# SyncE fetches the rows of ten tiles in one stream, 14 a step, in place of nine tiles with 13 rows a step

## The chip, the cores and the metric

One core of one Trainium2 chip. The metric is the time of the program on the device in microseconds (us), from the first to the last instruction with what lies around it. Lower is better. The engines are TensorE (PE; PEld is its weight load), VectorE (DVE), ScalarE (ACT), GpSimd (POOL) and SyncE (SP). A q behind a name (SPq, ACTq) means work of the sequencer, such as the issue of a DMA.

## What is computed

One layer of a graph network, its residual, and a layer norm. There are 6250 nodes of 128 features and 106250 edges of 64 features, sorted by target node.

```python
ef = relu(edge_attr @ We1 + be1) @ We2 + be2
ef = ef * sigmoid(timestamps[:, None] @ Wt + bt)
combined = concatenate([x[src], ef], axis=1)
msg = relu(combined @ Wn1 + bn1) @ Wn2 + bn2
out = segment_sum(msg, dst, num_segments=6250) + x
return layernorm(x + out)            # over the 128 features
```

## The kernel before

**Node table.** The part of Wn1 that acts on x[src] is applied to nodes, not to edges: `node_table` = x @ Wn1[:128] + bn1, one row of 128 float32 (512 bytes) a node. It is written to DRAM at the start. Wn2 is applied after the segment sum.

**Tiles.** A tile is 128 edges, one a partition. Four tiles are a group of 512 edges, two groups are a pair, and a pair is one step of the main loop. There are 104 pairs (`PAIRS`). The first four take their rows straight from x (gathered at the start), and the pairs 4 to 103 gather them from the node table. The buffer `gathered` holds four pairs (`BODY` = 4).

**Who does what in step s.** TensorE transposes the edge attributes of pair s into psT (L854, semaphore `eaT_ps`), sums the messages of pair s - 3 (L836), multiplies for pair s - 2 (L877), and makes the two edge layers of pair s (L890) and pair s - 1 (L902). ScalarE, in this order: copies sums, rectifies pair s - 3 (L621), places a fetched tile of pair s - 1 where there is one (`place_rows`, L598 and L602), copies the transposes (L655, `eaT_ready`, for which the first layer of this step and the transposes of the next wait), makes the sigmoid weights `tw` (L679), and rectifies the first layer (L687). VectorE adds the gathered rows of pair s - 2 (L1156, `pre_ready`), builds one-hot matrices and accumulates. In the steps that are multiples of four, ScalarE also stages a finished block of nodes (L715), and TensorE multiplies it in the step after.

**POOL** issues one indirect DMA for each tile, 128 rows each (L528), eight a pair. From pair 20 on (`CLOSE_FROM`) it begins pair p once L1156 of pair p - 2 is done (L539). One tile of some pairs, the last of its second group, is left out by POOL. The pairs in `FETCHED` (17, 27, ... 97, nine of them) have it fetched by SyncE, those in `ACT_FETCHED` (32, 54, 76, 98) by ScalarE's queue.

**SyncE** runs the steps n = 4 to 103 in the loop at the end of its program: wait until the transposes of step n - 4 are done, load the edge attributes of pair n (L438); `fetch_rows(n)`; wait until `tw` of step n - 4 is done, load the edge weights of pair n (L444). `fetch_rows` reads the node numbers of up to 13 edges into registers with one register load (`numbers_of`, L399) and issues for each edge a DMA of its own with one row of 512 bytes (L500). A tile takes the ten steps from p - 6 to p + 3, nine with 13 rows and one with 11. Steps 11 to 100 have rows. There are two buffers of one tile (`fetched`). Tile f waits at its first row until tile f - 2 has been placed (`placed`). `place_rows` on ScalarE waits for the 128 rows, which end in SyncE's step p + 3, and copies them into `gathered` in ScalarE's step p + 1. SyncE's loop runs up to four steps ahead of TensorE.

Of the kernel before, what the change touches and what calls it, by code (L numbers as in the profile page):

```python
# [43 lines left out]
SP_ENGINE = mybir.EngineType.SP  # L44

P = 128
# [30 lines left out]
CLOSE_FROM = 20  # L77


FETCH_ROWS, FETCH_STEPS = 13, 10  # L80
FETCHED = list(range(17, 98, FETCH_STEPS))


ACT_ROWS, ACT_STEPS, ACT_FROM = 6, 22, 10
# [3 lines left out]
def gnn_kernel(nc, x, src, dst, edge_attr, edge_weight, We1, be1, We2, be2, Wt, bt, Wn1, bn1, Wn2, bn2, out):  # L88
# [24 lines left out]
    table = nc.dram_tensor("node_table", (N, C), F32).ap()  # L113
    spans_dram = nc.dram_tensor("spans_dram", (G, 2), I32).ap()

    with ExitStack() as ctx:
        def sb(name, shape, dt=F32):
            return ctx.enter_context(nc.sbuf_tensor(name, shape, dt))
# [4 lines left out]
        def sem(name):  # L123
            return ctx.enter_context(nc.semaphore(name))
# [44 lines left out]
        fetched = sb("fetched", [P, 2, C])  # L169
# [47 lines left out]
        rows_in = [sem(f"rows_in{i}") for i in range(2)]  # L217
        placed, act_placed = sem("placed"), sem("act_placed")
# [74 lines left out]
        def wait_table(eng):  # L293

            for r, n in enumerate((RING, RING, len(BLOCKS) - 2 * RING)):
                eng.wait_ge(table_out[r], 16 * n)
# [99 lines left out]
        def numbers_of(engine, p, parts):  # L396

            g = p * PAIR + PAIR - 1
            return nc.values_load_multi_w_load_instructions(  # L399
                src_rows[g % P:g % P + 1, g // P, :].rearrange("a (p j) -> a j p", j=TILES)  # L400
                [:, ORDER[TILES - 1], parts.start:parts.stop], engines=(engine,), min_val=0, max_val=N - 1,
                skip_runtime_bounds_check_because="the edge's source node, which the inputs bound")[1]

        def by_group(a):

            return [a[E - SE:E].rearrange("(g e) -> g e", e=GE),
                    a[0:(P - SG) * GE].rearrange("(g e) -> g e", e=GE),
                    a[(P - SG) * GE:(G - SG) * GE].rearrange("(g e) -> g e", e=GE)]

        col, row = "(c a) -> c a", "(a c) -> a c"  # L410
# [11 lines left out]
        @block.sync  # L422
        def _(sp):
            def load_x(c):
                sp.dma_start(x_sb[:, c * XCH:(c + 1) * XCH, :],
                             x_blocks[:, c * XCH:(c + 1) * XCH, :]).then_inc(x_in[c], 16)

            def load_rows(tile, a, landed):
                last, first, second = by_group(a)
                for to, of in ((tile[0:SG, 0, :], last), (tile[SG:P, 0, :], first), (tile[0:ROWS[1], 1, :], second)):  # L430
                    sp.dma_start(to, of).then_inc(landed, 16)

            def edges_of(n):

                return (E - SE if n < 2 else (n // 2 - 1) * SE) + n % 2 * PE2

            def load_edges(n):
                sp.dma_start(ea[n // 2 % 2][:, n % 2 * PAIR:(n % 2 + 1) * PAIR, :],  # L438
                             edge_attr[bass.ds(edges_of(n), PE2), :].rearrange("(g p j) f -> p g (j f)", p=P, j=TILES))\
                    .then_inc(ea_in[n % BODY], 16)  # L440

            def load_weights_of(n):

                sp.dma_start(ew[n // 2 % 2][:, n % 2 * PAIR:(n % 2 + 1) * PAIR, :].rearrange("p g e -> p (g e)"),  # L444
                             edge_weight[bass.ds(edges_of(n), PE2)].rearrange("(a e) -> a e", a=1).to_broadcast([P, PE2]))\
                    .then_inc(ew_in[n % BODY], 16)

            def load_raw_e(n, a, b):

                part = src[E - SE:E] if a < SG else src[0:SE]  # L450
                sp.dma_start(raw_e[:, a:b, :], part.rearrange("(g p j) -> p g j", p=P, j=TILES)
                             [:, a % SG:(b - 1) % SG + 1, :]).then_inc(raw_e_in[n], 16)

            load_raw_e(0, 0, 2)
            for c in range(CHUNKS):
                load_x(c)
                if c == 1:
                    load_raw_e(1, 2, 4)
                if c == 3:
                    load_raw_e(2, 4, 8)  # L460
                    load_rows(src_rows, src, src_in)
            sp.dma_start(x_sb[0:LAST, FULL, 0:C], x_last).then_inc(x_in[CHUNKS], 16)
            load_rows(dst_rows, dst, dst_in)
            for to, of in loads_sp:
                sp.dma_start(to, of).then_inc(weights_in, 16)

            for b, (rows, n) in enumerate(BLOCKS):
                sp.wait_ge(table_ready, b + 1)
                sp.dma_start(table_blocks[:, b, :] if b < FULL else table_last,
                             table_sb[b][0:rows, 0:n * C]).then_inc(table_out[min(b // RING, 2)], 16)  # L470
                if b == RING:
                    load_edges(0)
                    load_edges(1)
            load_weights_of(0)
            load_weights_of(1)
            sp.wait_ge(span_ready, 2)
            for r in range(2):
                sp.dma_start(spans_dram[r * P:r * P + ROWS[r], :], span_i[0:ROWS[r], r, :]).then_inc(span_out, 16)
            load_edges(2)
            load_edges(3)  # L480
            sp.wait_ge(span_out, 32)
            sp.dma_start(spans[:, :, :], spans_dram.rearrange("(a g) k -> a g k", a=1)).then_inc(spans_in, 16)
            for to, of in loads_late:
                sp.dma_start(to, of).then_inc(late_in, 16)
            load_weights_of(2)
            load_weights_of(3)

            def fetch_rows(n):

                f, at = divmod(n - (FETCHED[0] - FETCH_STEPS + 4), FETCH_STEPS)  # L490
                if not 0 <= f < len(FETCHED) or at * FETCH_ROWS >= P:
                    return
                if f == 0 and at == 0:
                    wait_table(sp)
                if at == 0 and f > 1:
                    sp.wait_ge(placed, f - 1)
                parts = range(at * FETCH_ROWS, min((at + 1) * FETCH_ROWS, P))
                rows = numbers_of(SP_ENGINE, FETCHED[f], parts)
                for part, row in zip(parts, rows):
                    sp.dma_start(fetched[part:part + 1, f % 2, :], table[bass.ds(row, 1), :])\  # L500
                        .then_inc(rows_in[f % 2], 16)

            for n in range(BODY, PAIRS):
                sp.wait_ge(eaT_ps, n - BODY + 1)
                load_edges(n)
                if n == BODY:
                    sp.wait_ge(src_in, 48)
                fetch_rows(n)
                sp.wait_ge(tw_ready, n - BODY + 1)
                load_weights_of(n)  # L510
            sp.wait_ge(last.y_done, 1)
            sp.dma_start(out_last, x_sb[0:LAST, FULL, 0:C]).then_inc(y_out, 16)
# [3 lines left out]
        def _(pool):  # L516
# [20 lines left out]
            for p in range(RAW // PAIR, PAIRS):  # L537
# [6 lines left out]
                for q in range(PAIR):  # L544
                    for t in range(TILES):
                        if p in FETCHED + ACT_FETCHED and q * TILES + t == PAIR * TILES - 1:
                            continue
                        if p < PAIRS - 1:
                            landed = gather_in[p % BODY][0 if q * TILES + t < PART[0] else 1]
                        else:  # L550
                            landed = last_gather_in[0 if q == 0 else 1 + t]
                        gather_rows(gathered[:, p % BODY * PAIR + q, t * C:(t + 1) * C], table,
                                    src_e[:, p * PAIR + q, t:t + 1], landed,
                                    32 if p in FETCHED + ACT_FETCHED and q * TILES + t == PAIR * TILES - 2 else 16)


        @block.scalar
        def _(act):
# [32 lines left out]
            def place_rows(p):  # L591

                act.wait_ge(pre_ready, p - (BODY - 1))
                to = gathered[:, p % BODY * PAIR + PAIR - 1, (TILES - 1) * C:TILES * C]
                if p in FETCHED:
                    f = FETCHED.index(p)
# [889 lines left out]
```

## Time and profile before

| | us |
|---|---|
| median of 3 runs | 1047.69 (1046.63 to 1048.53) |
| the profiled execution | 1049.1 |
| its span | 1047.3 |
| TensorE busy | 855.0 (82%) |
| GpSimd busy | 779.7 (74%) |
| VectorE busy | 650.6 (62%) |
| ScalarE busy | 593.6 (57%) |
| mean granted clock of TensorE | 0.951 of full speed |

Busy time leaves out instructions that only wait, branch, load registers or issue DMAs. SyncE does nothing else, so it has no line here, and its work is seen only in the timeline. A row of a timeline merges instructions of one line that follow each other: its first number is the start, its second the time from the first's start to the last's end. The idle time in brackets is that ahead of the row, with what ended it.

### The profile page before, as it was taken

The numbers are of one execution on the slowest core, as the hardware profiler recorded it, in microseconds if no ns is written. First come the engines' busy times: TensorE is split into PE (matmuls) and PEld (weight loads), VectorE is DVE, ScalarE is ACT, GpSimd is POOL, SyncE is SP. The second block draws the span as 40 slices with busy tenths as digits, with TensorE's granted clock in tenths as the row PEclk, the third lists the DMA queues.
The fourth block names the chain that finished last, engine by engine and source line by source line (L and its number), as shares of the span: only waits on it lengthen the run. The fifth ranks groups of instructions, "written<-read, shape, count | busy, mean of one in ns | idle before, by whom it ended". The sixth has DMA issues, their size and how long they took to land.

```text
span 1047.3 us, 20873 instructions
## 1 busy us (share of the span) xinstructions
PE 855.0 (82%) x5031; PEld 624.6 (60%) x5032; DVE 650.6 (62%) x1688; ACT 593.6 (57%) x662; POOL 779.7 (74%) x828
## 2 busy tenths in 40 slices
PE   6999997988688888678778887887787786786884
PEld 6667675656566666465565655555565564564664
DVE  4767774765555765655466566566566556566566
ACT  5576664665365656555555555555565555654652
POOL 7777777777777777777777777777777777777773
PEclk9999998999888989989999999999999999999998
DMA  8964445444454444444444544444444444554321
GB/s 244 281 222 123 145 145 142 128 146 145 142 147 127 143 154 145 125 142 146 145 125 146 145 142 146 125 144 138 130 144 138 133 143 127 144 143 145 84 54 50
DMA packets 81709, 148.80 MB, mean 142 GB/s; under 512 B 20631, under 2 KB 50134, under 8 KB 81574
## 3 DMA queue, kind: packets, MB, share of 16 engines
q1 hardware_dynamic: 51750, 89.86, 27.6%
q0 software_dynamic: 26208, 53.73, 19.1%
q10 hardware_dynamic: 3616, 3.74, 1.1%
q8 instruction: 45, 0.74, 0.3%
q14 instruction: 90, 0.74, 0.2%
HBM read 140.85 MB, written 6.40 MB: 141 GB/s over the span
## 4 chain that ended last, share of the span: by engine, by line
POOL 47%; issue 22%; PE 13%; DMA 7%; DVE 6%; ACT 3%; ACTq 1%; SPq 1%; DVEq 1%; POOLq 0%
POOL gathered L528 47%; DMA gathered<-node_table,src_e 6%; PE psS L836 4%; PE psM L877 3%; DVE h L1156 2%; PE psE L902 2%; PE psH L890 2%; DMA x_sb<-in_x 1%; ACT h L621 1%; ACT tw L679 1%; DVE onehot L1162 1%; DVE efw L1177 1%; ACTq L617 0%; PE psS L821 0%; ACT h L687 0%
## 5 line engine op out<-in xcount | busy, mean ns | idle before, releaser
L528 POOL DMA_INDIRECT gathered<-node_table,src_e x787 | 748.0, 950 | 240.9 <-issue 234.1
L687 ACT ACTIVATE h<-psH,be_c 128x1024 f32<-128x1024 f32 x104 | 115.9, 1115 | 332.3 <-PE psH L890 329.3
L836 PE MATMUL psS<-onehot,h 128*128 128x128 f32 x1656 | 235.9, 300 | 76.1 <-ACT h L621 73.6
L836 PEld LDWEIGHTS psS<-onehot,h 128*128 128x128 f32 x1656 | 217.9, 211 | 94.9 <-issue 56.0
L1156 DVE TENSOR_TENSOR h<-psM,gathered 128x1024 f32<-128x1024 f32 (+1 forms) x104 | 122.7, 1182 | 227.9 <-DMA gathered<-node_table,src_e 169.6
L679 ACT ACTIVATE tw<-ew,bt_c,wt_c 128x1024 f32<-128x1024 f32 x104 | 235.5, 2265 | 18.1 <-DVE efw L1177 17.7
L877 PE MATMUL psM<-wn,efw 128*128 128x128 f32 x1664 | 210.6, 282 | 3.2 <-DVE h L1156 3.2
L902 PE MATMUL psE<-h,we 128*128 128x512 f32 x416 | 210.5, 629 | 0.0
L877 PEld LDWEIGHTS psM<-wn,efw 128*128 128x128 f32 x1664 | 203.1, 199 | 4.0 <-DVE h L1156 4.0
L1177 DVE SCALAR_TENSOR_TENSOR efw<-psE,be_c,tw 128x1024 f32<-128x1024 f32 x104 | 133.2, 1281 | 107.3 <-PE psE L902 106.7
L1162 DVE TENSOR_SCALAR onehot<-split_ids,dst_e 128x65 f32<-128x65 f32 x832 | 174.0, 272 | 0.0
L890 PE MATMUL psH<-eaT,we 64*128 64x512 f32 x416 | 121.1, 659 | 56.2 <-DMA gathered<-node_table,src_e 50.0
L902 PEld LDWEIGHTS psE<-h,we 128*128 128x128 f32 x416 | 72.4, 194 | 132.6 <-issue 132.6
L621 ACT ACTIVATE h<-h 128x1024 f32<-128x1024 f32 (+1 forms) x108 | 110.4, 1025 | 36.7 <-DVE h L1156 34.7
L1170 DVE TENSOR_REDUCE found<-onehot 128x128 f32<-128x512 f32 x104 | 109.9, 1056 | 3.6
L854 PEld LDWEIGHTS psT<-ident,ea 128*128 128x128 f32 x416 | 51.9, 141 | 53.0 <-issue 53.0
L890 PEld LDWEIGHTS psH<-eaT,we 64*128 64x128 f32 x416 | 31.8, 187 | 71.5 <-DMA gathered<-node_table,src_e 57.2
L1120 DVE TENSOR_TENSOR acc<-acc,found 128x128 f32 x204 | 58.3, 286 | 24.8 <-issue 18.2
L655 ACT ACTIVATE eaT<-psT 128x512 f32<-128x512 f32 x104 | 61.5, 591 | 7.9 <-PE psT L854 5.1
L854 PE MATMUL psT<-ident,ea 128*128 128x128 f32 x416 | 62.4, 273 | 0.0
L821 PE MATMUL psS<-wn,staged_own 128*128 128x128 f32 x88 | 20.2, 314 | 35.0 <-ACT h L621 35.0
L821 PEld LDWEIGHTS psS<-wn,staged_own 128*128 128x128 f32 x88 | 14.4, 205 | 39.8 <-issue 39.8
(113 smaller groups left out, 342.1 us busy)
## 6 DMA issues: line engine op xcount, KB each, us to landing
ew<-in_edge_weight SPq DMA_DIRECT2D x104, 512.0 KB, 4.2
ea<-in_edge_attr SPq DMA_DIRECT2D x104, 256.0 KB
fetched<-node_table SPq DMA_DIRECT2D x1152, 0.5 KB
gathered<-node_table,src_e POOLq DMA_INDIRECT x787, 2.5
raw_own<-node_table ACTq DMA_DIRECT2D x512, 0.5 KB
x_sb<-in_x SPq DMA_DIRECT2D x6, 512.0 KB, 8.9
out_y<-x_sb ACTq DMA_DIRECT2D x12, 256.0 KB
node_table<-gathered SPq DMA_DIRECT2D x7, 256.0 KB, 5.2
```

The source lines that it names most:

```text
L528: pool.indirect_dma_start(to, None, rows, bass.IndirectOffsetOnAxis(index, 0)).then_inc(landed, by)
L621: return nc.scalar.activation(at, at, ACT.Relu)
L679: nc.scalar.activation(tw[:, s % 2, :].rearrange("c (o i m) -> c o i m", o=2, i=2), ew[s // 2 % 2][:, s % 2 * PAIR:(s % 2 + 1) * PAIR, :] ...
L687: nc.scalar.activation(h1[:, s % 2, :], psH[:, :, :].rearrange("p r e -> p (r e)"), ACT.Relu, bias=be1_c[:, :]).then_inc(h1_ready, 1)
L836: return nc.tensor.matmul(to, h[:, (k - SUM_LAG) % BODY * PAIR + q, t * C:(t + 1) * C], hot, start=(t == 0), stop=(t == TILES - 1))
L854: mm = nc.tensor.transpose(psT[:, (a * PAIR + q) * P:(a * PAIR + q + 1) * P], ea[k // 2][:, k % 2 * PAIR + q, a * P:(a + 1) * P], ident[:, :])
L877: mm = nc.tensor.matmul(psM[:, q, t * P:(t + 1) * P], efw[:, (k - MSG_LAG) % 2, of], wn1[:, 1, :], start=True, stop=True)
L890: mm = nc.tensor.matmul(psH[:, a, :], we1[a * F:(a + 1) * F, :], eaT[a * F:(a + 1) * F, k % 2, :], start=True, stop=True)
L902: mm = nc.tensor.matmul(psE[:, r, :], we2[:, :], h1[:, (k - EF_LAG) % 2, r * GE:(r + 1) * GE], start=True, stop=True)
L1156: return nc.vector.tensor_tensor(to, of, rows, ALU.add)
L1162: made = nc.vector.tensor_scalar(onehot[:, (k - MSG_LAG) % 2, q * TILES + t, :].rearrange("p (a b) -> p a b", b=IDS), split_ids[:, :, 0:ID ...
L1177: nc.vector.scalar_tensor_tensor(efw[:, (k - EF_LAG) % 2, :], psE[:, :, :].rearrange("p r e -> p (r e)"), be2_c[:, :], tw[:, (k - EF_LAG) ...
```

## The change

`FETCH_ROWS` goes from 13 to 14. The fetching no longer starts anew every ten steps. From step 11 on, the rows of all tiles are one stream, 14 a step, and a step in which one tile ends fetches the first rows of the next as well, with a register load for each of the two. There are ten tiles. `FETCHED` becomes 17, 26, 35, 44, 53, 62, 71, 81, 90, 99. The last row (number 1279) is in step 102. POOL leaves out the tiles of the ten pairs.

```diff
-FETCH_ROWS, FETCH_STEPS = 13, 10
-FETCHED = list(range(17, 98, FETCH_STEPS))
+FETCH_ROWS, FETCH_FROM, FETCH_TILES = 14, 11, 10
+FETCHED = [FETCH_FROM + (-(-(f + 1) * P // FETCH_ROWS)) - 4 for f in range(FETCH_TILES)]
```

```diff
             def fetch_rows(n):
 
-                f, at = divmod(n - (FETCHED[0] - FETCH_STEPS + 4), FETCH_STEPS)
-                if not 0 <= f < len(FETCHED) or at * FETCH_ROWS >= P:
-                    return
-                if f == 0 and at == 0:
+                first = (n - FETCH_FROM) * FETCH_ROWS
+                if n == FETCH_FROM:
                     wait_table(sp)
-                if at == 0 and f > 1:
-                    sp.wait_ge(placed, f - 1)
-                parts = range(at * FETCH_ROWS, min((at + 1) * FETCH_ROWS, P))
-                rows = numbers_of(SP_ENGINE, FETCHED[f], parts)
-                for part, row in zip(parts, rows):
-                    sp.dma_start(fetched[part:part + 1, f % 2, :], table[bass.ds(row, 1), :])\
-                        .then_inc(rows_in[f % 2], 16)
+                for f in range(FETCH_TILES):
+                    parts = range(max(first - f * P, 0), min(first + FETCH_ROWS - f * P, P))
+                    if n < FETCH_FROM or not parts:
+                        continue
+                    if parts.start == 0 and f > 1:
+                        sp.wait_ge(placed, f - 1)
+                    rows = numbers_of(SP_ENGINE, FETCHED[f], parts)
+                    for part, row in zip(parts, rows):
+                        sp.dma_start(fetched[part:part + 1, f % 2, :], table[bass.ds(row, 1), :])\
+                            .then_inc(rows_in[f % 2], 16)
```

## Rows read from the trace of the kernel before

**Rows 1.** The page: the span.
```profile
span 1047.3 us, 20873 instructions
```

**Rows 2.** The page: the chain that ended last, share of the span by engine.
```profile
POOL 47%; issue 22%; PE 13%; DMA 7%; DVE 6%; ACT 3%; ACTq 1%; SPq 1%; DVEq 1%; POOLq 0%
```

**Rows 3.** Line L528: ns min/median/max, first and last start us.
```profile
L528 POOL DMA_INDIRECT gathered<-node_table,src_e x787: 942/947/1470, 43.6 to 1031.2; - x197
```

**Rows 4.** Timeline of SyncE, steps 11 and 12: start us, us, what.
```profile
85.69 0.38 SPq L438 DMA_DIRECT2D ea<-in_edge_attr  x1
89.23 5.66 SPq L500 DMA_DIRECT2D fetched<-node_table  x13
...
95.35 0.55 SPq L438 DMA_DIRECT2D ea<-in_edge_attr  x1
```

**Rows 5.** Timeline of SyncE: starts of steps 21, 30 (whole), 31, 51, 61.
```profile
179.23 0.42 SPq L438 DMA_DIRECT2D ea<-in_edge_attr  x1
...
264.36 0.42 SPq L438 DMA_DIRECT2D ea<-in_edge_attr  x1
267.55 4.45 SPq L500 DMA_DIRECT2D fetched<-node_table  x11
272.05 0.37 SPq L444 DMA_DIRECT2D ew<-in_edge_weight  x1
272.47 0.43 SPq L438 DMA_DIRECT2D ea<-in_edge_attr  x1
...
461.08 0.43 SPq L438 DMA_DIRECT2D ea<-in_edge_attr  x1
...
556.07 1.74 SPq L438 DMA_DIRECT2D ea<-in_edge_attr  x1
```

**Rows 6.** Lines L399 (SyncE 13 or 11, ScalarE 6 values), L371 (one), L500: ns.
```profile
L399 SPq TENSOR_LOAD <-src_rows x90: 2454/2916/3962, 86.2 to 939.1; - x90
...
L399 ACTq TENSOR_LOAD <-src_rows x10: 1475/1482/1492, 108.9 to 186.8; - x10
...
L371 DVEq TENSOR_LOAD <-lowest x50: 305/315/326, 70.2 to 1024.3; - x50
...
L500 SPq DMA_DIRECT2D fetched<-node_table x1152: 224/228/314, 89.2 to 946.0; - x192
```

**Rows 7.** Timeline of TensorE: transposes of steps 17 and 94.
```profile
159.38 0.60 PE L854 MATMUL psT<-ident,ea 128*128 128x128 f32 x4
...
919.51 0.60 PE L854 MATMUL psT<-ident,ea 128*128 128x128 f32 x4
```

**Rows 8.** Timeline of SyncE: weights of step 97, start of 98, rows of 100.
```profile
919.02 0.37 SPq L444 DMA_DIRECT2D ew<-in_edge_weight  x1
920.14 0.41 SPq L438 DMA_DIRECT2D ea<-in_edge_attr  x1
...
941.72 4.47 SPq L500 DMA_DIRECT2D fetched<-node_table  x11
```

**Rows 9.** Waits of SyncE: us in total, times, longest us.
```profile
SPq L438 <- PE psT L854: 45.3, 22, 9.2
```

**Rows 10.** Waits of all engines: ScalarE's copy of fetched rows.
```profile
ACT gathered L598 <- DMA fetched<-node_table: 13.3, 2, 7.3
```

**Rows 11.** Timeline of ScalarE: copies of the tiles of pairs 17, 27, 97.
```profile
179.81 0.31 ACT L598 ACTIVATE gathered<-fetched 128x128 f32<-128x128 f32 x1 [7.25 <-DMA fetched<-node_table]
...
273.09 0.31 ACT L598 ACTIVATE gathered<-fetched 128x128 f32<-128x128 f32 x1 [6.04 <-DMA fetched<-node_table]
...
962.32 0.29 ACT L598 ACTIVATE gathered<-fetched 128x128 f32<-128x128 f32 x1
```

**Rows 12.** Timeline: VectorE's L1156 of pairs 27 and 99, POOL's start of pair 101.
```profile
287.34 1.23 DVE L1156 TENSOR_TENSOR h<-psM,gathered 128x1024 f32<-128x1024 f32 x1 [0.26 <-PE psM L877]
...
994.73 1.22 DVE L1156 TENSOR_TENSOR h<-psM,gathered 128x1024 f32<-128x1024 f32 x1 [3.86 <-PE psM L877]
...
1002.27 0.95 POOL L528 DMA_INDIRECT gathered<-node_table,src_e  x1 [0.31 <-issue]
```

## The prediction

> **What bounds the kernel now.** I read the span first [rows 1], then the chain that ended last [rows 2]. Its largest shares are POOL's gathers of L528 and "issue", the pause that stands between two of them. The row of that line says the same in another way [rows 3]: 787 gathers start between 43.6 and 1031.2 us, so 987.6 / 786 = 1.256 us from one to the next, with hardly a hole. So POOL sets the end today, and one gather is worth 1.256 us. A pair of groups needs 8 gathers, or 7 where SyncE or ScalarE fetches one tile row by row. Over 100 pairs with 13 such tiles that is 7.87 x 1.256 = 9.88 us a pair.
>
> The second thing to look at is SyncE, which no view of busy time shows. Its timeline gives the time at which it issues the load of edge attributes of step n (L438); between that and the load of weights (L444) stand the rows of a tile. I call the start of that first load A(n). A(11) = 85.69 [rows 4]. A tile is ten steps, nine with 13 rows and one with 11, so the next tiles open at A(21) = 179.23, A(31) = 272.47, and later ones at A(51) = 461.08 and A(61) = 556.07 [rows 5]. The first tile therefore takes SyncE 93.5 us, the second 93.2, the fifth 95.0, and one on average (556.07 - 85.69) / 5 = 94.1, or 9.41 us a step. Is it waiting in there, or is that its own work? L438 waits until the transposes of step n - 4 have ended. Those of step 17 end at 159.38 + 0.60 = 159.98 [rows 7], and A(21) is 19.2 us later. So there SyncE waits for nobody, it is late by itself. At step 98 it is different: weights issued 919.02, transposes of step 94 ended 920.11, A(98) = 920.14 [rows 7, 8]. Late in the kernel it waits at nearly each step, 45.3 us in sum over the whole run [rows 9]. In short: SyncE at 9.41 us a step is just faster than POOL at 9.88, with 5% to spare.
>
> And its lateness has a path to the end. A tile fetched for pair p has its last rows issued in SyncE's step p + 3, and ScalarE copies it in its own step p + 1 (L598), ahead of the copies and activations that all other engines need. That copy waited twice, 13.3 us in all [rows 10]: for pair 17 at 179.81 and for pair 27 at 273.09 [rows 11]. The last one, for pair 97, did not wait: rows out at 941.72 + 4.47 = 946.19 [rows 8], copied at 962.32 [rows 11]. POOL did not feel the two waits, since it was ahead.
>
> **The change, part by part.**
> 1. One gather fewer (14 tiles are fetched by rows in place of 13): -1.26 us on POOL, which counts only as long as POOL sets the end.
> 2. 128 more rows for SyncE, 1280 in place of 1152, and the steps with rows go from 90 to 92 (11 to 102). Price of one more row in a step, from durations: a DMA issue, 4.45 / 11 = 0.405 us [rows 5]; one more value in the register load of L399, (2.916 - 1.482) / (13 - 6) = 0.205 us, where the 6-value load is ScalarE's [rows 6]. Sum 0.61. From whole steps: step 30 with 11 rows takes 272.47 - 264.36 = 8.11, the nine before it with 13 rows take (264.36 - 179.23) / 9 = 9.46, so 0.67 a row [rows 5]. I take 0.62, near the first, as the second also holds an irregular slow issue that is not a matter of one row.
> 3. Steps that cross the end of a tile load numbers twice. Of nine crossings one falls on a step's edge (7 x 128 = 64 x 14), so eight. No row shows a split load; its bounds are nothing, and the shortest load seen, one value for VectorE, 0.315 us [rows 6]. 2.916 - 13 x 0.205 leaves 0.25 fixed; I take 0.2 each, 1.6 us. The added wait for the copy of the tile before last costs an instruction: that copy is 9 steps old.
> 4. The due point does not move: with the new list a tile for pair p still ends in SyncE's step p + 3, the last one (pair 99) in step 102, with 6 rows.
>
> The Trainium skill (page "DMA: Bandwidth & Descriptors", section "Latency and other measured facts") gives a register load a floor of some 600 ns. The one-value load at 0.315 us speaks against that here. By the page the eight splits would cost 4.8 us in place of 1.6, and the time would be 3 us longer.
>
> **The sum.** A step has a fixed part a, and b for each row. Ten steps with 128 rows take 10a + 128b = 94.08. From A(11) to A(102) there are 91 steps with 91 x 14 = 1274 rows: 91a + 1274b = 91 x 9.408 + (1274 - 1164.8) b = 856.1 + 109.2 x 0.62 = 923.8 us. That is 10.15 us a step, above POOL's 7.86 x 1.256 = 9.87. So SyncE waits nowhere any more, and the sum can be made along it alone: A(102) = 85.69 + 923.8 + 1.6 = 1011.1. Then the issue of that load 0.42, the load of 6 numbers 1.48, 6 rows 2.43: last row out at 1015.4. From the last row out to the copy: 273.09 - 272.00 = 1.1 [rows 5, 11]. From the copy's start to the end of VectorE's L1156 for the same pair: 287.34 + 1.23 - 273.09 = 15.5 [rows 11, 12]. This is for step 28; step 100, where pair 99 is copied, is a multiple of four as well, so the same staging of a block lies in it (a bound from below is about 12, as I take that block work out). So L1156 of pair 99 ends at 1032.0, against 994.73 + 1.22 = 995.95 now. POOL may gather pair 101 only after that (L539). It starts it at 1002.27 now [rows 12], 6.3 us after; then at once, at 1032.1. From there everything to the end is the same 24 gathers and the same tail: 1047.3 - 1002.3 = 45.0. New span 1077.1, which is +29.8. The profiled execution took 1049.1 us with a span of 1047.3, so 1.8 lie around it, and 1078.9 comes out. It is 1.4 above the median of the runs, so the forecast for the median is 1077.5 us.
>
> What is queued behind the waiting instruction on ScalarE: the copy of the transposed edges, the sigmoid and both rectifiers of the step. TensorE waits for those, VectorE for TensorE, and POOL for L1156 two pairs back. So everything stands still once a tile, first lightly (pair 26), later more each tile: nine steps take SyncE 91.4 us, and nine pairs with one tile by rows take POOL 71 x 1.256 = 89.2.
>
> **Rivals.**
> Not slower. The extra row is mostly hidden, and SyncE stays ahead of POOL. It decides at A(102): for POOL to start pair 101 at 1001.0, A(102) must be 1001.0 - 0.1 - 15.5 - 1.1 - 4.3 = 980.0, so 91 steps in 894.3 us, 9.83 a step. By the formula that needs b = 0.35, and both ways of reading b give over 0.6; against it. For it: the DMA instruction of a row alone has a median of 0.228 us [rows 6], the rest of the 0.405 lies between the instructions; but even that with 0.205 for the number makes 0.43, so this end is not reached either. Then the gather saved is all: 1047.69 - 1.26 = 1046.4, which is within the 0.2% that a measurement of this kernel tells from no change. The Trainium skill (same page, section "Anatomy of one DMA — SWDGE (gpsimd) path") has about 50 ns for the sequencer's dispatch of a DMA; with a load of 0.205 beside it this would be b = 0.26, and this rival would be the truth. The x11 row with 0.405 us a DMA speaks against it. Chance 0.04 for no difference, 0.01 for faster.
>
> Slower, but less. Every tile goes at the pace of the second one, 93.24 in place of 94.08, which takes 9.1 x 0.84 = 7.6 us off, and the way from copy to L1156 is 12 in place of 15.5: 1077.5 - 7.6 - 3.5 = 1066. For it: SyncE's slow tiles lie in the middle, and I don't know their cause. Chance 0.2.
>
> Slower, and more. Every tile goes at the pace of the fifth, 94.99: +8.3; b is 0.67: +5.5: 1091. TensorE, which stands still more often, may also be granted less clock; no bound from these rows. Chance 0.2.
>
> The forecast has 0.5, and 0.05 is left for something in which SyncE falls back still more.
>
> **How the numbers follow.** The range goes from 1064 to 1092, which takes in both slower rivals. Faster by over 0.2% 0.01, within 0.2% 0.04, slower 0.95.
>
> **What the new profile would show.** SyncE's step from L438 to L438 with 14 rows about 10.1 us (13 rows: 9.46), with no wait for L854 after step 12. A(102) near 1011. The wait of L598 for rows in most of the ten copies, far above 13.3 us. POOL no longer without holes: idle before L528 with L1156 as releaser, and the start of the last 24 gathers near 1032. I am wrong in the step price if the 14-row step is under 9.8 us, wrong in the path if A(102) is late and POOL is not, and wrong in the tail if more than 46 us lie behind the start of pair 101.

## The result, and the profile after

The changed kernel takes 1080.91 us (median of 6 runs, 1076.97 to 1084.08), against 1046.98 us for the kernel before (6 runs). The ratio is 1.0321, with a 95% interval of 1.0307 to 1.0336. It is 3.2% slower. The profiled execution took 1081.46 us with a span of 1079.7.

Line numbers of the new kernel are one higher from `fetch_rows` on: L501 are the row DMAs of SyncE, L529 the gathers, L599 the copy of fetched rows, L656 the copy of the transposed edges, L680 the sigmoid, L855 TensorE's transposes, L1157 the add of the gathered rows.

First the page of the changed kernel: its span, and the chain that ended last by engine.

```profile
span 1079.7 us, 21268 instructions
...
SPq 53%; issue 16%; PE 15%; DVE 6%; ACT 4%; DMA 2%; POOL 2%; ACTq 1%; DVEq 1%; POOLq 0%
SPq L501 27%; SPq L399 20%; PE psS L837 4%; PE psE L903 4%; PE psM L878 3%; SPq L438 3%; PE psH L891 3%; SPq L444 2%; POOL gathered L529 2%; ACT h L622 1%; DMA x_sb<-in_x 1%; ACT tw L680 1%; DMA fetched<-node_table 1%; DVE onehot L1163 1%; DVE h L1157 1%
```

POOL had 47% of this chain [rows 2] and has 2%; SyncE's sequencer, absent before but for 1%, has 53%: row DMAs and the register loads of their numbers.

Next the waits (us in total, times, longest us), of all engines and then of SyncE.

```profile
ACT gathered L599 <- DMA fetched<-node_table: 103.5, 10, 14.3
...
POOL gathered L529 <- DVE h L1157: 40.3, 24, 7.0
```

```profile
SPq L438 <- PE psT L855: 14.9, 7, 4.3
```

ScalarE's copy now waits at every one of the ten tiles, 103.5 us in sum, where it waited twice for 13.3 [rows 10]. The waits do not grow from tile to tile: they lie between 3.8 and 14.3 us, with 9.0 us at the first tile and 13.0 at the last. POOL stands still behind VectorE's add for 40.3 us, where it stood for 6.8 in the kernel before. SyncE waits for TensorE 14.9 us in place of 45.3 [rows 9], and all of that but 1.1 us lies before its first rows: from step 12 on it is 3 to 31 us behind the transposes that it might have to wait for.

The timeline of SyncE (start us, us), steps 11 and 12, then the last two with rows, 101 and 102:

```profile
88.54 0.38 SPq L438 DMA_DIRECT2D ea<-in_edge_attr  x1
92.29 6.07 SPq L501 DMA_DIRECT2D fetched<-node_table  x14
98.40 0.37 SPq L444 DMA_DIRECT2D ew<-in_edge_weight  x1
98.81 0.43 SPq L438 DMA_DIRECT2D ea<-in_edge_attr  x1
102.54 5.68 SPq L501 DMA_DIRECT2D fetched<-node_table  x14
...
999.94 0.44 SPq L438 DMA_DIRECT2D ea<-in_edge_attr  x1
1003.66 5.68 SPq L501 DMA_DIRECT2D fetched<-node_table  x14
1009.39 0.37 SPq L444 DMA_DIRECT2D ew<-in_edge_weight  x1
1009.80 0.42 SPq L438 DMA_DIRECT2D ea<-in_edge_attr  x1
1011.94 2.70 SPq L501 DMA_DIRECT2D fetched<-node_table  x6
1014.68 0.37 SPq L444 DMA_DIRECT2D ew<-in_edge_weight  x1
1015.10 0.43 SPq L438 DMA_DIRECT2D ea<-in_edge_attr  x1
```

The last row of pair 99's tile is out at 1014.64. What follows from it is in the timeline of all engines. I leave out what is not on the way to POOL:

```profile
1015.69 0.31 ACT L599 ACTIVATE gathered<-fetched 128x128 f32<-128x128 f32 x1 [12.98 <-DMA fetched<-node_table]
1015.90 0.58 ACT L656 ACTIVATE eaT<-psT 128x512 f32<-128x512 f32 x1
...
1016.63 2.08 PE L891 MATMUL psH<-eaT,we 64*128 64x512 f32 x4 [10.03 <-ACT eaT L656]
...
1018.63 3.42 PE L903 MATMUL psE<-h,we 128*128 128x512 f32 x4
...
1026.37 1.95 PE L878 MATMUL psM<-wn,efw 128*128 128x128 f32 x16
...
1028.35 1.23 DVE L1157 TENSOR_TENSOR h<-psM,gathered 128x1024 f32<-128x1024 f32 x1 [0.76 <-PE psM L878]
...
1030.35 0.95 POOL L529 DMA_INDIRECT gathered<-node_table,src_e  x1 [4.21 <-DVE h L1157]
```

The brackets tell the story in one place: 13 us of ScalarE's wait, then TensorE's 10 us behind it, then POOL's 4.2 us. POOL starts pair 101 at 1030.35 and not at 1002.27 [rows 12]. The same point for other pairs shows how it grew: POOL is later than before by 2.7 us at pair 19, 6.3 at 28, 11.6 at 37, 14.2 at 46 and at 55, 19.0 at 64, 25.1 at 73, 24.3 at 83 and at 92, 28.1 at 101 (starts of its gathers in both timelines). The first 2.7 us are not the work of the fetched tiles. POOL is 2.9 us late already at pair 8, ahead of SyncE's first rows. The first gather of pair 8 before and after:

```profile
84.28 0.95 POOL L528 DMA_INDIRECT gathered<-node_table,src_e  x1 [0.99 <-DVE h L1156]
...
87.14 0.94 POOL L529 DMA_INDIRECT gathered<-node_table,src_e  x1 [4.05 <-DVE h L1157]
```

### The profile page after: what moved, and what is told of

Its sections match the earlier page's. It is cut to its first block, busy times and chain, and to the rows that moved or that the text cites. A ratio compares the mean times of both kernels' runs of the same rounds, so it can differ in the third digit from the quotient of the medians.

```text
span 1079.7 us, 21268 instructions
## 1 busy us (share of the span) xinstructions
PE 863.8 (80%) x5031; PEld 623.9 (58%) x5032; DVE 650.5 (60%) x1688; ACT 594.7 (55%) x663; POOL 775.9 (72%) x827
## 4 chain that ended last, share of the span: by engine, by line
SPq 53%; issue 16%; PE 15%; DVE 6%; ACT 4%; DMA 2%; POOL 2%; ACTq 1%; DVEq 1%; POOLq 0%
SPq L501 27%; SPq L399 20%; PE psS L837 4%; PE psE L903 4%; PE psM L878 3%; SPq L438 3%; PE psH L891 3%; SPq L444 2%; POOL gathered L529 2%; ACT h L622 1%; DMA x_sb<-in_x 1%; ACT tw L680 1%; DMA fetched<-node_table 1%; DVE onehot L1163 1%; DVE h L1157 1%
## 5 line engine op out<-in xcount | busy, mean ns | idle before, releaser
L529 POOL DMA_INDIRECT gathered<-node_table,src_e x786 | 744.3, 947 | 272.8 <-issue 232.5
L837 PE MATMUL psS<-onehot,h 128*128 128x128 f32 x1656 | 227.0, 293 | 65.2 <-ACT h L622 62.8
L837 PEld LDWEIGHTS psS<-onehot,h 128*128 128x128 f32 x1656 | 209.6, 204 | 82.8 <-issue 55.0
L680 ACT ACTIVATE tw<-ew,bt_c,wt_c 128x1024 f32<-128x1024 f32 x104 | 235.3, 2264 | 21.2 <-DVE efw L1178 16.7
L1157 DVE TENSOR_TENSOR h<-psM,gathered 128x1024 f32<-128x1024 f32 (+1 forms) x104 | 122.6, 1182 | 171.0 <-DMA gathered<-node_table,src_e 117.4
L903 PE MATMUL psE<-h,we 128*128 128x512 f32 x416 | 223.6, 663 | 0.0
L878 PE MATMUL psM<-wn,efw 128*128 128x128 f32 x1664 | 212.9, 284 | 5.6 <-DVE h L1157 5.6
L878 PEld LDWEIGHTS psM<-wn,efw 128*128 128x128 f32 x1664 | 205.3, 201 | 6.5 <-DVE h L1157 6.5
L891 PE MATMUL psH<-eaT,we 64*128 64x512 f32 x416 | 126.0, 684 | 83.9 <-ACT eaT L656 67.7
L903 PEld LDWEIGHTS psE<-h,we 128*128 128x128 f32 x416 | 75.7, 202 | 139.9 <-issue 139.9
L891 PEld LDWEIGHTS psH<-eaT,we 64*128 64x128 f32 x416 | 33.4, 195 | 97.7 <-issue 69.3
L855 PEld LDWEIGHTS psT<-ident,ea 128*128 128x128 f32 x416 | 53.7, 145 | 57.9 <-issue 57.9
L656 ACT ACTIVATE eaT<-psT 128x512 f32<-128x512 f32 x104 | 61.6, 592 | 12.5 <-PE psT L855 10.0
L855 PE MATMUL psT<-ident,ea 128*128 128x128 f32 x416 | 63.5, 276 | 0.0
L599 ACT ACTIVATE gathered<-fetched 128x128 f32<-128x128 f32 x10 | 3.1, 309 | 103.5 <-DMA fetched<-node_table 103.5
```

Of the source, the lines that this page charges most:

```text
L529: pool.indirect_dma_start(to, None, rows, bass.IndirectOffsetOnAxis(index, 0)).then_inc(landed, by)
L680: nc.scalar.activation(tw[:, s % 2, :].rearrange("c (o i m) -> c o i m", o=2, i=2), ew[s // 2 % 2][:, s % 2 * PAIR:(s % 2 + 1) * PAIR, :] ...
L837: return nc.tensor.matmul(to, h[:, (k - SUM_LAG) % BODY * PAIR + q, t * C:(t + 1) * C], hot, start=(t == 0), stop=(t == TILES - 1))
L878: mm = nc.tensor.matmul(psM[:, q, t * P:(t + 1) * P], efw[:, (k - MSG_LAG) % 2, of], wn1[:, 1, :], start=True, stop=True)
L891: mm = nc.tensor.matmul(psH[:, a, :], we1[a * F:(a + 1) * F, :], eaT[a * F:(a + 1) * F, k % 2, :], start=True, stop=True)
L903: mm = nc.tensor.matmul(psE[:, r, :], we2[:, :], h1[:, (k - EF_LAG) % 2, r * GE:(r + 1) * GE], start=True, stop=True)
```

## Experiments

The theory: a step of SyncE with 14 rows takes longer than a pair takes POOL, and SyncE's lateness reaches all others through ScalarE's copy. Two rivals: traffic of the additional DMAs (T), and the new places of the tiles (L). Each kernel was timed together with the kernel before, and the ratios are to that.

**1. All DMAs, no numbers to load.**

```diff
-                    rows = numbers_of(SP_ENGINE, FETCHED[f], parts)
-                    for part, row in zip(parts, rows):
-                        sp.dma_start(fetched[part:part + 1, f % 2, :], table[bass.ds(row, 1), :])\
+                    for part in parts:
+                        row = (part * 47 + f * 611) % N
+                        sp.dma_start(fetched[part:part + 1, f % 2, :], table[row:row + 1, :])\
                             .then_inc(rows_in[f % 2], 16)
```

> The changed kernel without SyncE's register loads (L399): each of the 1280 row DMAs has a fixed row number, so the same number of DMAs of 512 bytes go to the same places at the same steps, but the ten tiles hold the wrong rows of the node table. Theory (SyncE's time a step sets the end, through ScalarE's copy of the rows): a step of SyncE falls from 10.1 us by the load's 3.2 us to about 6.9, SyncE is ahead of POOL again, ScalarE's copy waits for rows at most for the first tile, and the time is that of POOL with 786 gathers, 1045 to 1047 us. Rival T (the traffic of the 128 more row DMAs, or their packets in the queue, slows gathers and loads): the DMAs are all there, so it stays near 1081. Rival L (the new places of the tiles, 53 beside 54 and 98 beside 99, and the last one so near the end): it stays near 1081.

Measured: 1048.17 us, ratio 0.999 (0.9979 to 1.000). Its chain by engine, and SyncE's wait for TensorE:

```profile
POOL 50%; issue 22%; PE 9%; DMA 8%; DVE 7%; ACT 2%; SPq 1%; DVEq 1%; ACTq 0%; POOLq 0%
```

```profile
SPq L438 <- PE psT L855: 415.9, 96, 8.5
```

With every DMA and every place of the changed kernel, the whole loss is gone. SyncE waits 415.9 us for TensorE, and POOL is back in the chain with 50%. Both rivals fall: neither the traffic nor the places cost anything that can be measured, as long as SyncE is in time. The edit takes more off SyncE than I had expected. A DMA whose address is fixed is also issued faster than one whose address is in a register: 14 of them take 4.15 us in the step below, in place of 5.68.

```profile
173.40 0.40 SPq L438 DMA_DIRECT2D ea<-in_edge_attr  x1
173.83 4.15 SPq L501 DMA_DIRECT2D fetched<-node_table  x14
```

So SyncE's own work in a step was near 5 us and not 6.9.

**2. Nothing but SyncE's work.** The kernel before, and one more number and one more DMA a step:

```diff
+                first = min(parts.start, P - len(parts) - 1)
-                rows = numbers_of(SP_ENGINE, FETCHED[f], parts)
+                rows = numbers_of(SP_ENGINE, FETCHED[f], range(first, first + len(parts) + 1))
+                rows = rows if first == parts.start else rows[1:] + rows[:1]
                 for part, row in zip(parts, rows):
                     sp.dma_start(fetched[part:part + 1, f % 2, :], table[bass.ds(row, 1), :])\
                         .then_inc(rows_in[f % 2], 16)
+                sp.dma_start(spare_rows[n:n + 1, :], table[bass.ds(rows[len(parts)], 1), :]).then_inc(spare_in, 16)
```

> The kernel before with its nine tiles at their places; in each of the 90 steps with rows SyncE loads one more number and issues one more row DMA, into a buffer that nobody reads. Theory: 0.62 us a step more, 90 x 0.62 = 56 us, of which SyncE's waits took up some 45. From the rate of the changed kernel the rows of pair 97 are out near 990, its copy is at 991 in place of 962, L1156 of pair 97 ends near 1003 and POOL starts pair 99 there in place of 982.3: about 21 us longer, 1064 to 1072. Rival L (places of the tiles): nothing of it is changed here, 1047. Rival T (traffic): 90 DMAs of 512 bytes in 149 MB, so at most what the 128 of the change brought by it.

Measured: 1068.86 us, ratio 1.0183 (1.0166 to 1.0200). From step 11 (86.50) to step 100 it takes 10.00 us a step. The total is as expected, but it did not come together at the last tile as my text has it: the rows of pair 97 were copied at 986.48, 4.5 us earlier than I had them, and POOL, 19.5 us late already at pair 89, added 0.6 us to that by pair 99. The waits, and SyncE's last step with rows beside the copy of pair 97:

```profile
ACT gathered L604 <- DMA fetched<-node_table: 93.1, 9, 13.7
```

```profile
976.56 0.42 SPq L440 DMA_DIRECT2D ea<-in_edge_attr  x1
980.55 4.80 SPq L504 DMA_DIRECT2D fetched<-node_table  x11
```

```profile
986.48 0.31 ACT L604 ACTIVATE gathered<-fetched 128x128 f32<-128x128 f32 x1 [6.65 <-DMA fetched<-node_table]
```

The copy stood at 962.32 in the kernel before [rows 11]. Tiles, places and gathers are those of before, so 20 us come from SyncE's work alone.

**3. and 4. The halves of that row.** Only the DMA, with a number that is loaded anyway (first diff), and only the number (second):

```diff
+                for q in range(1):
+                    sp.dma_start(spare_rows[n:n + 1, q, :], table[bass.ds(own[q], 1), :]).then_inc(spare_in, 16)
```

```diff
-                rows = numbers_of(SP_ENGINE, FETCHED[f], parts)
...
+                first = min(parts.start, P - len(parts) - 1)
+                rows = numbers_of(SP_ENGINE, FETCHED[f], range(first, first + len(parts) + 1))
```

> The kernel before; in each of the 90 steps with rows SyncE issues one more row DMA into a buffer that nobody reads, with a node number that it has already loaded. That is one half of spare_row: the issue, 0.405 us, without the number. Theory: SyncE's step goes from 9.41 to 9.82 us, still under POOL's 9.88. SyncE falls back by 19 us less than in spare_row (its step 100 starts near 957, the rows of pair 97 are copied near 968), and that is just in time for POOL: 1047 to 1053 us. If each row DMA costs in proportion, whatever the bound, this would be two thirds of spare_row's 20 us: 1061.

> The kernel before; SyncE's register load of each step reads one number more (14 in place of 13) and nothing is issued for it. The other half of spare_row, 0.205 us. Theory: SyncE's step is 9.61 us, under POOL's 9.88: 1047 to 1050 us. If it costs in proportion: 1055.

Measured: the DMA alone 1052.97 us, ratio 1.0040 (1.0025 to 1.0055); the number alone 1049.43 us, ratio 1.0020 (1.0004 to 1.0036). Together they would be 0.6%, and both at once gave 1.83%. So the cost is not in proportion. It sets in when SyncE's step passes POOL's pace of 9.88 us: over the steps 11 to 61 it measured 9.58 us with the number alone, 9.79 with the DMA alone and 9.99 with both, against 9.41 in the kernel before. The bend is not sharp, as a tile can be late at one place while the mean still fits: ScalarE's copy waited 28.8 us in sum with the number alone and 40.8 with the DMA alone. In the trace with the DMA alone POOL fell back by 5.5 us between pair 19 and pair 29, over the first two tiles, and by nothing after that.

**5. The stream without the 14th row.** Nine tiles:

```diff
-FETCH_ROWS, FETCH_FROM, FETCH_TILES = 14, 11, 10
+FETCH_ROWS, FETCH_FROM, FETCH_TILES = 13, 12, 9
```

> The changed kernel with 13 rows a step and nine tiles, its stream from step 12 on (so that no tile falls on one of ScalarE's): the stream over tile ends and the split register loads are kept, the 14th row and the tenth tile are not. Theory: a step of SyncE takes 9.5 us, 9.88 is what POOL needs, so POOL sets the end as before: 1046 to 1050 us. Rival (it is the split loads or the wait for the copy of the tile before last at a tile's first row that hold SyncE up): clearly above 1055.

Measured: 1049.58 us, ratio 1.0002 (0.9989 to 1.0014). The stream over the ends of tiles, its split loads and its added waits cost nothing that can be measured.

**6. 14 rows, but no tenth tile.**

```diff
-FETCH_ROWS, FETCH_FROM, FETCH_TILES = 14, 11, 10
+FETCH_ROWS, FETCH_FROM, FETCH_TILES = 14, 11, 9
```

> The changed kernel without its tenth tile (pair 99), still 14 rows a step up to step 93. Theory: up to pair 92 nothing changes, whose gathers start at 939.0 in the changed kernel; after that POOL runs on without a hole, 95 gathers at 1.25 us, and with a tail of 16 us the span is 1073, the time about 1074, that is 7 us less than the changed kernel and 27 above before, though POOL gathers as much as before. Rival L (the last tile is too near the end, and the other nine cost little): 1047 to 1055.

Measured: 1074.65 us, ratio 1.0244 (1.0220 to 1.0269). The last tile has 6 us of the loss by the medians and 8 by the ratios, the nine ahead of it the rest. SyncE fetches as many rows here as in the kernel before and POOL makes as many gathers; what is new is that a tile of 128 rows is due every nine steps or so and not every ten. For 9.14 pairs POOL takes 90.2 us, and SyncE needs 92.5 for as many steps with 14 rows.

**7. The tiles placed three pairs later.** SyncE's instructions stay as they are:

```diff
-FETCHED = [FETCH_FROM + (-(-(f + 1) * P // FETCH_ROWS)) - 4 for f in range(FETCH_TILES)]
+FETCHED = [FETCH_FROM + (-(-(f + 1) * P // FETCH_ROWS)) - 1 for f in range(FETCH_TILES)]
```

> The changed kernel with the fetched tiles given to pairs three later each (20, 29, ... 102 in place of 17, 26, ... 99); SyncE's program is the same instruction for instruction, only the number of the pair differs. So ScalarE's copy in step p + 1 now follows SyncE's step p by one and no longer comes three steps ahead of it. Theory: the wait of the copy goes, but SyncE still needs 10.12 us a step against POOL's 9.87 and its last loads of weights come as late as before: for pair 102 issued near 1014.7, landed 4.2 later at 1018.9, where ScalarE used them at 999.1 in the kernel before. So part of the loss stays: 1056 to 1067 us. If the copy were the only path from SyncE to the end, the time would be POOL's, 1046 to 1049 us. If the places had nothing to do with it, 1081.

Measured: 1072.99 us, ratio 1.0233 (1.0212 to 1.0254). No copy waits any more, and another wait stands in its place:

```profile
ACT tw L680 <- DMA ew<-in_edge_weight: 165.1, 76, 4.7
...
POOL gathered L529 <- DVE h L1157: 29.5, 26, 4.2
```

The kind of answer was right, the size was not: I had at most 1067. ScalarE's rows near the end show why:

```profile
1016.21 2.24 ACT L680 ACTIVATE tw<-ew,bt_c,wt_c 128x1024 f32<-128x1024 f32 x1 [2.75 <-DMA ew<-in_edge_weight]
...
1024.24 2.27 ACT L680 ACTIVATE tw<-ew,bt_c,wt_c 128x1024 f32<-128x1024 f32 x1 [0.30 <-DVE efw L1178]
```

I reckoned that the sigmoid of pair 102 starts when its weights have landed. But the one of pair 101 waited until 1016.21, and a step of TensorE and VectorE lies between the two. So pair 102's starts at 1024.24, 47.0 us ahead of the end of the span (1071.2), as in the changed kernel (1032.70 to 1079.7).

**8. Weights issued ahead of the rows, too.**

```diff
-                fetch_rows(n)
                 sp.wait_ge(tw_ready, n - BODY + 1)
                 load_weights_of(n)
+                fetch_rows(n)
```

> As late_place, with the load of weights issued ahead of the step's rows and not behind them. Theory: the weights of pair 102 are issued near 1010.2 in place of 1014.7 and those of the steps before about 9.3 us earlier; the last pairs gain some 4 to 5 us on late_place. If it is the load of attributes or SyncE's waits that hold the end, and not the weights, the same as late_place.

Measured: 1072.35 us, ratio 1.0232 (1.0208 to 1.0256): no gain on the one before, where I expected 4 to 5 us. The wait moved once more, to the load that now comes last in SyncE's step:

```profile
PE psT L855 <- DMA ea<-in_edge_attr: 119.4, 62, 3.8
...
ACT tw L680 <- DMA ew<-in_edge_weight: 21.3, 40, 1.7
```

So here the order within SyncE's step decides only who waits. SyncE's start of step 103 is at 1023.9 here and was at 1017.9 in run 7; its step was 10.24 us on average (steps 11 to 102) against 10.17. Why the same instructions take longer in this order I did not try to find out.

**9. and 10. Ten tiles within SyncE's time.** The rows are spread over all steps from 8 to 102 (13 or 14 in each), each tile is placed in the step of its last row, and the weights go first:

```diff
+FETCH_FROM, FETCH_TO, FETCH_TILES = 8, 103, 10
+def first_row(n):
+    return (n - FETCH_FROM) * FETCH_TILES * P // (FETCH_TO - FETCH_FROM)
+FETCHED = [next(n for n in range(FETCH_FROM, FETCH_TO) if first_row(n + 1) >= (f + 1) * P) + 0
+           for f in range(FETCH_TILES)]
...
-                first = (n - FETCH_FROM) * FETCH_ROWS
+                first, last = first_row(n), first_row(n + 1)
...
-                fetch_rows(n)
                 sp.wait_ge(tw_ready, n - BODY + 1)
                 load_weights_of(n)
+                fetch_rows(n)
```

> Ten tiles, but the 1280 rows spread evenly over SyncE's steps 8 to 102 (13 or 14 a step, 13.47 in the mean), each tile for the pair in whose step its last row is issued (17, 26, 36, 45, 55, 64, 74, 83, 93, 102), and the weights issued ahead of the rows. SyncE is done with its rows at A(8) + 95 x 1.47 + 1280 x 0.62 = 65.5 + 933 = 999, 9.82 us a step, below POOL's 9.87. Theory: POOL sets the end with 786 gathers, 1.26 us below the kernel before, a ratio of 0.9988 (0.997 to 1.001). If SyncE has less to spare than the sum says: 1.002 to 1.01.

> As even10, and ScalarE's queue fetches five tiles in place of four: 7 rows a step in place of 6, a tile in 19 steps, from step 6 on, for pairs 25, 44, 63, 82, 101. POOL has 785 gathers. Theory: as long as ScalarE's step stays under POOL's 9.86 us, another 1.25 us less than even10, a ratio of 0.9976 to the kernel before. Rival: ScalarE's step, which has 5.7 us of activations and 6 rows with their load of 3.9 us already, gets 0.6 us longer and sets the pace in TensorE's waits: slower than even10, 1.00 to 1.02.

Measured: even10 1047.98 us, ratio 0.9991 (0.9977 to 1.0004); with ScalarE's fifth tile (`ACT_ROWS, ACT_STEPS, ACT_FROM = 7, 19, 6`) 1047.62 us, ratio 0.9995 (0.9984 to 1.0005). POOL has 51% of the first one's chain, and SyncE none. SyncE's step is 9.84 us (steps 11 to 102), where I had 9.82. So ten tiles fit, if SyncE begins three steps earlier and takes 13.5 rows a step. Run 8 is the one to compare with: it has the late places and the weights first as well, and lost 2.3%. Whether those two are needed for the result, no run tells. The gain of a gather, 0.12% by the sum, is inside the interval of the first. The 0.24% expected of two lies outside that of the second, so the fifth tile did not bring what I expected, and why stays open. Neither is shown to be faster than the kernel before. I did not find a version that is.

## Why the prediction was right

The forecast was 1077.5 us, slower; 1080.9 was measured. Its steps, one by one, against the trace of the changed kernel:

| term | predicted | measured |
|---|---|---|
| A(11), the first step with rows | 85.7 | 88.5 |
| 91 steps to A(102) | 925.4 | 921.3 |
| from A(102) to the last row out | 4.3 | 4.8 |
| last row out to ScalarE's copy | 1.1 | 1.05 |
| copy to the end of L1157 of pair 99 | 15.5 | 13.9 |
| from there to POOL's start of pair 101 | 0.1 | 0.8 |
| from there to the end of the span | 45.0 | 49.35 |
| span | 1077.1 | 1079.7 |

**SyncE's step.** 921.3 / 91 = 10.12 us, 10.17 expected with the splits. The price of a row, 0.62 us, held nearly: over the steps 11 to 61 one DMA and one number more moved the step from 9.41 to 9.99 us, the DMA alone by 0.38 and the number alone by 0.17. The median of L399 agrees in kind (100 loads, 3.077 us, where 90 had 2.916 [rows 6], so 0.16 for the 14th value). The Trainium skill (page "DMA: Bandwidth & Descriptors", section "Latency and other measured facts") gives some 600 ns as the least for a register load. This case's traces do not agree: the smallest load in stream13 took 479 ns. Eight of its loads are there because of splits, and it took no longer than the kernel before:

```profile
L399 SPq TENSOR_LOAD <-src_rows x97: 479/2882/3657, 97.5 to 946.3; - x97
```

**The path through ScalarE's copy.** As predicted, it decides in this kernel. But it is not the only one there is. Run 7, without it, is only 8 us shorter and waits for the weights; in run 8 the attributes take their place. My text had SyncE's lateness reach the end by one way; it reaches it by each load that SyncE issues.

**POOL's lateness, tile by tile.** I had POOL fall back by the difference of the paces (91.4 against 89.2 us for nine steps); the starts of POOL's gathers show a growth of 3.6, 5.3, 2.6, 0, 4.8 and 6.1 us from tile to tile up to pair 73, none up to pair 92, and then 3.8. I also had the standstill get longer with each tile ("first lightly (pair 26), later more"). It did not: ScalarE's wait was 9.0 us for pair 17, 13.6 for pair 26 and 14.3 for pair 35, and never longer after. The steps are uneven in part because the way from copy to L1157 is longer where a block is finished (steps that are a multiple of four): 16.8 us for pair 35 and 16.4 for pair 71, against 11.7 to 12.4 for pairs 17, 53, 81 and 90. But pair 44 has 16.2 without a block and pair 99 only 13.9 with one, so this is not all of it. A smaller slip stands beside it: I had SyncE wait at nearly each step late in the kernel before, and its row has 22 waits in all [rows 9].

**The term that was mis-sized: the tail.** I said that behind POOL's start of pair 101 everything stays as it was, 45.0 us. It is 49.35. In the kernel before, POOL began pair 101 6.3 us after L1156 of pair 99 had ended [rows 12]. In the changed one it begins 0.8 us after. TensorE's three steps from pair 99 to pair 102 start at the same point in both, L1157 of pair 99, and so they lie 5.6 us later against POOL. L1157 of pair 102 in the changed kernel, the rectifier behind it, and POOL's last gather:

```profile
1057.78 1.21 DVE L1157 TENSOR_TENSOR h<-psM,gathered 128x1024 f32<-128x1024 f32 x1
...
1059.02 1.06 ACT L622 ACTIVATE h<-h 128x1024 f32<-128x1024 f32 x1 [8.80 <-DVE h L1157]
...
1059.23 0.95 POOL L529 DMA_INDIRECT gathered<-node_table,src_e  x1 [0.30 <-issue]
```

And L1156 of pair 102 in the kernel before:

```profile
1025.33 1.21 DVE L1156 TENSOR_TENSOR h<-psM,gathered 128x1024 f32<-128x1024 f32 x1
```

From POOL's start of pair 101 to this instruction it was 23.1 us and is 27.4. From there to the end it is 22.0 and 21.9. So the 4.35 us are TensorE's way over three pairs, which POOL's 24 gathers had covered. A sum along one engine has to ask at each switch what else started at the same moment. No run was made for this reading, but the traces of the others bear it out. In runs 7 and 8 POOL also begins pair 101 0.8 us after L1157 of pair 99, and 49.3 us lie behind it in both. In stream13, nine14, spare_row, spare_dma and spare_number it begins 5.6 to 7.5 us after, and 44.7 to 44.9 lie behind it. const_rows lies between, with 3.8 and 46.3. The end of L1157 of pair 99 and POOL's start of pair 101 in run 7, whose span is 1071.2:

```profile
1019.88 1.23 DVE L1157 TENSOR_TENSOR h<-psM,gathered 128x1024 f32<-128x1024 f32 x1 [4.65 <-PE psM L878]
...
1021.88 0.94 POOL L529 DMA_INDIRECT gathered<-node_table,src_e  x1 [1.73 <-DVE h L1157]
```

**Errors that cancelled.** A(11) was 2.9 us later and the 91 steps 4.1 us shorter. The way from the copy to L1157 was 1.6 us shorter and the tail 4.35 longer. That the span came within 2.6 us of the forecast is in part luck. The lateness of A(11) comes from the start of the program, where step 8 was at 62.75 in one trace and at 65.53 in the other; over the traces of all kernels here A(8) lies between 62.8 and 66.9. Such a scatter reaches POOL, too. In stream13, where A(8) was 66.93, POOL began pair 8 at 88.32 and pair 101 at 1005.90, 3.6 us later than in the kernel before, though POOL sets the end in both. So 3 us of difference between two single traces mean nothing here.

**The rivals.** "Not slower" would have needed b = 0.35; b is about 0.6. The dispatch of some 50 ns that the page "DMA: Bandwidth & Descriptors" of the Trainium skill gives (section "Anatomy of one DMA — SWDGE (gpsimd) path") is given for GpSimd's path, and it is not the price of a DMA in a row of them on SyncE: 14 took 5.68 us, 0.406 each. "Slower, but less" counted on 93.24 us a tile, so 917.8 for the 91 steps, and 12 from copy to L1157; "slower, and more" on 94.99 and b = 0.67, so 939.2, and on TensorE's clock. With 921.3 and 13.9 the runs lie between the forecast and the first of the two. The granted clock did fall, from 0.951 to 0.921 of full speed in the mean, but the way from copy to L1157 was shorter than I had it.

## What to carry to other kernels

An engine that only issues DMAs has no busy time, and still has a pace: take the start of its first instruction in each step, over ten steps or more, and set it beside the pace of the engine in the chain. Here they stood at 9.41 and 9.88 us, and 0.7 us more on the first turned a saving of 1.26 us into a loss of 34. When such an engine is late, later places and another order mostly shift who waits: later places took back 8 us of the 34, the other order nothing. The work in its step has to go down. In even10 it did, as the same rows were spread over more steps from an earlier start, and the loss was gone.

## What the runs showed of the hardware

- One more DMA of 512 bytes in a row of DMAs with a register address costs SyncE 0.41 us by its timeline (14 in 5.68 us) and 0.38 a step in spare_dma. With a fixed address it is 0.30 (const_rows, 14 in 4.18 us in the median). One more value in a register load of 13 costs 0.16 to 0.2 us (medians of L399) and 0.17 a step in spare_number. The two add up: with both, in spare_row, the step was 0.58 us longer.
- After TensorE had stood still for 10.03 us behind a copy, its next eight matmuls ran at little over half speed. L891 took 2.08 us in place of 1.13, and L903 3.42 in place of 1.98. L891 took 2.08 us behind eight of the ten copies of the changed kernel. The first row is the stretch of the wait, the second those matmuls, the third what comes after. The number behind the five engines is the mean granted clock of the stretch: 0.54, close to the level of 1.2 GHz, and then 1.00, that of 2.4 GHz.

```profile
1005.00:1016.00 11.00, 1.60 (x15) 1.41 (x13) 2.05 (x2) 0.31 (x2) 8.35 (x9) 0.79 0.47 129
1016.50:1022.00 5.50, 5.37 (x9) 2.04 (x10) 0.00 (x0) 5.33 (x5) 4.28 (x5) 0.54 0.83 275
1024.00:1030.00 6.00, 6.00 (x45) 4.88 (x44) 4.27 (x12) 2.31 (x2) 1.83 (x2) 1.00 0.12 33
```
